# A decoder layer on one core: softmax results turned by VectorE blocks and DMAs through DRAM instead of TensorE transposes

## The chip, the cores and the metric

The kernel runs on one core of a Trainium2 chip. The metric is the time of one execution on the device in microseconds, lower is better. The core has five engines with a queue of instructions each: TensorE (PE, matrix products; PEld are its weight loads), VectorE (DVE), ScalarE (ACT), GpSimd (POOL) and SyncE (SP), which here issues every DMA. Engines wait for each other through semaphores. A DMA adds 16 to its semaphore when it has landed. Products of TensorE land in PSUM, eight banks of 128 x 512 floats; all else lies in SBUF or in DRAM.

## The reference

Eight batches of 128 rows of 512 floats. Three layers, each added to its input: an attention of one head, a cross attention of 32 heads, and a feed forward with a small mixture of low-rank experts. The change is in the cross attention. With `x` normalised and `c` the context, for each head h:

```python
h_q = (x @ w_q.T).reshape(b, lq, H, DH)
h_k = (key_value_states @ w_k.T).reshape(b, lk, H, DH)
h_v = (key_value_states @ w_v.T).reshape(b, lk, H, DH)
score = einsum('bqhd,bkhd->bhqk', h_q, h_k) + position_bias[None]
score = softmax(where(m, score, -inf), axis=-1)
attn = einsum('bhqk,bkhd->bqhd', score, h_v).reshape(b, lq, H * DH)
out = hidden_states + attn @ w_out.T
```

For the product with `h_v` TensorE wants the softmax result of each batch, a 128 x 128 tile with a query in each partition, with a key in each partition: it has to be turned.

## The kernel before, in words

Heads are worked in 16 pairs (`GROUPS`; `PAIR` = 2, head `j` = 0 or 1 of pair `g`). Keys and values of all pairs are projected in a first stage and kept in DRAM (`keys`, `values`); the queries of a pair are projected in the loop, in seven products of a Strassen-like scheme (`project_queries`, slots 0 to 6). Every large product is done in three passes of high and low parts (`three_pass`, L573). The values are written to DRAM in blocks: `turn_blocks` (L1349) turns each 32 x 32 block inside a 128 x 512 tile on VectorE, `store_values` writes them in runs of 128 bytes, `load_values` reads runs of 512 bytes, and so the tile comes back turned as a whole.

Each engine has its order written out by hand, in a function `pair(g)` of its own. On TensorE a pair is: slots 0 to 3 of the queries; the transposes of the probabilities of head (g-1, 1) (`turn_head_probs`, L637); slots 4 to 6; the scores of head (g, 0) (L627); the values of head (g-1, 1) weighed with them (`weigh_head_values`, L645); the scores of head (g, 1); the output products of pair g-1 for six of the eight batches (`project_out`, 48 products in all, in two banks `VO` in turn); the transposes of head (g, 0); the last two batches; the values of head (g, 0).

Between scores and transposes a head goes through `take_scores` (VectorE adds bias and mask, L1210), `maxima` (L1215), `exponentials` (ScalarE, L899), `row_scales` (VectorE, L1229 and L1231) and `normalise_probs` (GpSimd, L534). After the transposes, ScalarE and VectorE copy a bank each to `probs_t` (`copy_probs_t`, L905 and L1236). The weighed values are split into high and low parts (`split_head_out`, L910 and L1241), and `add_out` (L1143) adds the output products to `acc`.

SP issues the DMAs of a pair in `refill(g)`, each behind the wait that frees its buffer: the query weights of the next pair (`fetch_heads`), its bias, the values of this pair (`load_values`, four DMAs of 256 KB), the keys of the next (`load_keys`, 1 MB) and its output weights (`fetch_out`). SP's waits are in order: what stands behind a wait is issued after it.

Of the kernel before, what the change touches and what calls it, by code (L numbers as in the profile page):

```python
# [8 lines left out]
F32 = mybir.dt.float32  # L9
# [3 lines left out]
B = 8  # L13
# [43 lines left out]
def decoder_kernel(nc, x, ctx_t, mask, w_qkv, b_qkv, w_o, b_o, ln_w, pos_bias, weights, w_base, w_routed, w_lora_b,  # L57
                   out):
    with ExitStack() as ctx:
# [63 lines left out]
        probs_t = put("probs_t", ctx_at + 8 * KB, [P, B, P])  # L123
# [33 lines left out]
        beats, ties = (probs_t[:, n:n + 2, :].rearrange("p b (e j) -> p (b e) j", j=NE) for n in (0, 2))  # L157
# [31 lines left out]
        v_loaded = sem("v_loaded")  # L189
        stored = sem("stored")  # L190
# [56 lines left out]
        probs_turned = sem("probs_turned")  # L247
        probs_t0_copied = sem("probs_t0_copied")
# [36 lines left out]
        def _(sp):  # L285
# [105 lines left out]

            fetch_bias(1)
# [3 lines left out]
            fetch_heads(0, 1, Q_COLS)  # L396
            sp.wait_ge(wo_lo_ready, 1)
            fetch_out(1)
            sp.wait_ge(k_stored, 16 * (GROUPS - 2))
            sp.wait_ge(product_done, SLOTS * (K1 + 1))  # L400
            n = 0
            for src, width in ((w_base, KC * C), (w_routed, KC * ROUTED), (w_lora_b, C)):
                sp.dma_start(ffn_raw[:, n:n + width], src).then_inc(ffn_loaded, 16)
                n += width

            def refill(g, last=False):
# [12 lines left out]

            with sp.Fori(1, GROUPS - 1) as g:  # L420
                refill(g)
# [8 lines left out]
        def _(pool):  # L430
# [100 lines left out]
            def normalise_probs(g, j):  # L531
                for i in range(2):
                    pool.wait_ge(scale_ready, 2 * (PAIR * g + j) + i + 1)
                    pool.tensor_tensor(probs[j][:, half(i), :], probs[j][:, half(i), :],  # L534
                                       row_scale[:, j, half(i)].unsqueeze(2).to_broadcast([P, HALF, P]),
                                       ALU.mult).then_inc(probs_ready, 1)
# [30 lines left out]
        def _(pe):  # L567
# [121 lines left out]
            def head_scores(g, j):  # L689
                s = PAIR * g + j + 1  # L690
                for i in range(2):
# [3 lines left out]
            def turn_head_probs(g, j):  # L695
                pe.wait_ge(ot_lo_ready, 2 * (PAIR * g + j + 1))
                turn_probs(PAIR * g + j + 1, probs[j])

            def weigh_head_values(g, j):
                pe.wait_ge(v_loaded, 64 * g + 64)  # L700
                weigh_values(PAIR * g + j + 1, lambda b: v[:, j, b, :], probs_t)

            def project_out(g, some):
                pe.wait_ge(wo_lo_ready, g + 1)
                for b in some:
                    if b % HALF == 0:
                        pe.wait_ge(ot_lo_ready, 2 + 2 * PAIR * g + 3 + b // HALF)
                    pe.wait_ge(out_added, B * (g + 1) + b - 1)
                    three_pass(VO[b % 2][:, :],
                               [([s[:, j, cols(b)] for s in ot], [s[:, j, :] for s in wo])  # L710
                                for j in range(PAIR)]).then_inc(out_done, 1)
# [53 lines left out]
            turn_head_probs(0, 0)  # L765
            weigh_head_values(0, 0)
# [22 lines left out]
            def last_out():  # L789
                g = GROUPS - 1  # L790

                def part(b, j):
                    return three_pass(LAST_OUT[b][:, :], [([s[:, j, cols(b)] for s in ot], [s[:, j, :] for s in wo])],
                                      start=(j == 0), stop=(j == 1))

                pe.wait_ge(wo_lo_ready, GROUPS)
                pe.wait_ge(scores_biased, 2 * HEADS + 2)
                pe.wait_ge(ot_lo_ready, 2 * HEADS)
                pe.wait_ge(dve_took, 3 * (FIRST + GROUPS))
                pe.wait_ge(act_took, 4 * (FIRST + GROUPS))  # L800
                part(0, 0)
                part(1, 0)
                turn_head_probs(g, 1)
                part(2, 0)
                part(3, 0)
                weigh_head_values(g, 1)
                pe.wait_ge(out_added, B * GROUPS)
                part(4, 0)
                part(5, 0)
                for b in range(B):  # L810
# [61 lines left out]
        def _(act):  # L872
# [198 lines left out]

            act.wait_ge(scores_done, 6)
            take(K1, 0, kt)
            take(K1, 1, kt)
            exponentials(1, 0, probs[0], 0)
            take(K1, 2, kt)
            exponentials(1, 0, probs[0], 1)
            high_for_queries(1, (0, 1))
            take(K1, 3, kt)
            high_for_queries(1, (2, 3))  # L1080
            copy_probs_t(1, probs_t)
            exponentials(2, 1, probs[1], 0)
            split_head_out(0, 0)
# [3 lines left out]
            def pair(g, last=False):  # L1087
# [6 lines left out]
                copy_probs_t(PAIR * g, probs_t)  # L1094
# [12 lines left out]
                copy_probs_t(PAIR * g + 1, probs_t)  # L1107
                act.wait_ge(out_done, B * (g + 1))
                high_out(g)
                split_head_out(g, 0)  # L1110
# [7 lines left out]
            copy_probs_t(HEADS, probs_t)  # L1118
# [20 lines left out]
        def _(dve):  # L1139
            def add_out(n, b, banks=None):  # L1140
                dve.wait_ge(out_done, B * n + b + 1)
                of = (banks or VO * HALF)[b]
                dve.tensor_tensor(acc[:, b, :], of[:, :], acc[:, b, :], ALU.add).then_inc(out_added, 1)  # L1143
# [61 lines left out]
            def take_scores(g, j, i):  # L1205
                s = PAIR * g + j + 1
                dve.wait_ge(scores_done, 2 * s + i + 1)
                if i == 0:
                    dve.wait_ge(bias_mask_ready, s)
                dve.tensor_tensor(probs[j][:, half(i), :], tiles(SC[i]), bias_mask[j][:, half(i), :],  # L1210
# [248 lines left out]
            take(K1, 0, kt)  # L1459
            take(K1, 1, kt)  # L1460
            row_scales(0, 0, 0)
            row_scales(0, 0, 1)
            take(K1, 2, kt)
            low_for_queries(1, 0)
            low_for_queries(1, 1)
            copy_probs_t(1, probs_t)
            low_for_queries(1, 2)
            split_head_out(0, 0)
            low_for_queries(1, 3)
            row_scales(0, 1, 0)  # L1470
            row_scales(0, 1, 1)

            def pair(g, last=False):
                n = FIRST + g
                take(n, 0, qt)
                copy_probs_t(PAIR * g, probs_t)
# [11 lines left out]
                for b in range(B):  # L1488
                    add_out(g, b)
                    if b < 2:  # L1490
                        row_scales(g, 0, b)
                    elif b in (2, 3, 4, 6) and not last:
                        low_for_queries(g + 1, (2, 3, 4, 6).index(b))
                    if b in (4, 5):
                        row_scales(g, 1, b - 4)
                    if b == 5:
                        copy_probs_t(PAIR * g + 1, probs_t)
                split_head_out(g, 0)

            with dve.Fori(1, GROUPS - 1) as g:  # L1500
                pair(g)
            pair(GROUPS - 1, last=True)
            copy_probs_t(HEADS, probs_t)
# [145 lines left out]
```

## Time and profile before

| | |
|---|---|
| median of 3 runs | 924.11 us (923.15 to 924.11) |
| profiled execution | 926.98 us, its span 925.3 us |
| TensorE busy | 876.8 us, 95% |
| VectorE busy | 627.8 us, 68% |
| ScalarE busy | 424.4 us, 46% |
| GpSimd busy | 354.0 us, 38% |
| mean granted TensorE clock | 0.991 |
| DMA | 108.52 MB, 117 GB/s over the span |

The span runs from the first to the last instruction of the profiled execution; its own time is 1.7 us longer. A busy share is that of the whole span. Times in the sections below are microseconds from the start of the span.

### The profile page before, as it was taken

How to read it: one execution, taken by the hardware profiler on the slowest of the kernel's cores; microseconds unless marked ns; L12 is line 12 of the kernel's file. 1: busy time of each engine (PE TensorE's matmuls, PEld its weight loads, DVE VectorE, ACT ScalarE, POOL GpSimd, SP SyncE). 2: the span in 40 equal slices, each digit the busy share in tenths (PEclk: the TensorE clock that was granted, in tenths of full speed). 3: DMA queues.
4: the chain of work that ended last, by engine and by line, in shares of the span. 5: the costliest groups of instructions: out<-in, count | busy, mean ns of one | idle time of the engine just before them, and what ended most of it. 6: DMA issues, size and time to landing. Idle time of an engine off the chain costs nothing.

```text
span 925.3 us, 14534 instructions
## 1 busy us (share of the span) xinstructions
PE 876.8 (95%) x4528; PEld 734.8 (79%) x4528; DVE 627.8 (68%) x1086; ACT 424.4 (46%) x1091; POOL 354.0 (38%) x328
## 2 busy tenths in 40 slices
PE   5799998999999999987999999999999999999898
PEld 4677786877777887776888888888888888888697
DVE  7877775677777676566557766677656766576554
ACT  3543443664444344354545553454535554454220
POOL 3312334232443232243764355544554345642100
PEclk9999999999999999999999999999999999999899
DMA  8026565556667657617334342434325352442002
GB/s 272 12 92 153 143 137 140 133 149 157 151 147 183 174 141 141 139 48 175 84 110 128 104 132 71 132 97 135 100 93 136 96 142 74 118 113 45 1 1 91
DMA packets 207661, 108.52 MB, mean 117 GB/s; under 512 B 136592, under 2 KB 187920, under 8 KB 203920
## 3 DMA queue, kind: packets, MB, share of 16 engines
q1 hardware_dynamic: 207632, 108.16, 45.1%
q8 instruction: 15, 0.25, 0.1%
q14 instruction: 14, 0.11, 0.0%
HBM read 74.58 MB, written 33.55 MB: 117 GB/s over the span
## 4 chain that ended last, share of the span: by engine, by line
PE 81%; DVE 10%; issue 3%; POOL 3%; ACT 2%; DMA 1%; SPq 0%; DVEq 0%; ACTq 0%; POOLq 0%
PE bank L573 64%; PE bank L627 6%; PE bank L645 6%; PE bank L637 3%; DVE w_lo L1257 2%; DVE st L1266 1%; DVE turned L1349 1%; PE bank L591 1%; POOL w_sum L477 1%; DMA raw_a<-in_w_qkv 1%; DVE stats L1150 1%; POOL rstd L456 1%; POOL w_sum L475 1%; DVE acc L1143 1%; ACT st L953 1%
## 5 line engine op out<-in xcount | busy, mean ns | idle before, releaser
L953 ACT COPY st<-bank 128x512 f32<-128x512 f32 x192 | 112.2, 587 | 266.0 <-PE bank L573 259.6
L573 PE MATMUL bank<-ctx_hi,w_hi 128*128 128x512 f32 x448 | 179.3, 400 | 16.4 <-DVE st L1266 8.6
L1266 DVE TENSOR_TENSOR st<-bank,st 128x512 f32<-128x512 f32 x144 | 98.4, 689 | 124.9 <-PE bank L573 124.7
L573 PE MATMUL bank<-ctx_lo,w_hi 128*128 128x512 f32 x448 | 174.7, 390 | 0.0
L573 PE MATMUL bank<-ctx_hi,w_lo 128*128 128x512 f32 x448 | 174.7, 390 | 0.0
L475 POOL TENSOR_TENSOR w_sum<-raw 128x256 f32<-128x256 f32 x48 | 39.4, 820 | 251.4 <-PE bank L573 224.0
L534 POOL TENSOR_TENSOR probs<-probs,row_scale 128x512 f32<-128x512 f32 x64 | 66.6, 1040 | 175.7 <-DVE row_scale L1231 172.7
L573 PEld LDWEIGHTS bank<-ctx_hi,w_hi 128*128 128x128 f32 x448 | 84.0, 188 | 46.8 <-issue 11.7
L573 PE MATMUL bank<-wo_hi,ot_hi 128*128 128x512 f32 x256 | 105.3, 412 | 6.5 <-issue 4.7
L1143 DVE TENSOR_TENSOR acc<-bank,acc 128x512 f32<-128x512 f32 x136 | 93.6, 690 | 20.7 <-PE bank L573 18.7
L899 ACT ACTIVATE probs<-probs,neg_max 128x128 f32<-128x128 f32 x264 | 102.4, 392 | 1.1 <-DVE neg_max L1215 1.1
L573 PE MATMUL bank<-wo_lo,ot_hi 128*128 128x512 f32 x256 | 100.9, 394 | 0.0
L573 PE MATMUL bank<-wo_hi,ot_lo 128*128 128x512 f32 x256 | 100.8, 394 | 0.0
L573 PEld LDWEIGHTS bank<-ctx_hi,w_lo 128*128 128x128 f32 x448 | 84.1, 188 | 18.0
L1257 DVE TENSOR_TENSOR w_lo<-w_sum,w_hi 128x512 fp32r<-128x512 f32 x96 | 79.7, 840 | 25.3 <-POOL w_sum L481 19.9
L573 PEld LDWEIGHTS bank<-ctx_lo,w_hi 128*128 128x128 f32 x448 | 84.2, 188 | 15.8
L573 PE MATMUL bank<-x_hi,w_hi 128*128 128x512 f32 x224 | 90.5, 404 | 1.8 <-ACT st L953 1.8
L573 PE MATMUL bank<-x_hi,w_lo 128*128 128x512 f32 x224 | 87.6, 391 | 0.0
L573 PE MATMUL bank<-x_lo,w_hi 128*128 128x512 f32 x224 | 87.6, 391 | 0.0
L498 POOL TENSOR_TENSOR bias_mask<-mask_add,bias 128x1024 f32<-128x1024 f32 x32 | 77.0, 2422 | 11.1 <-DVE probs L1210 11.1
L1257 DVE TENSOR_TENSOR w_lo<-raw,w_hi 128x256 fp32r<-128x256 f32 x96 | 60.1, 626 | 23.2 <-ACT w_hi L945 23.2
L945 ACT CAST w_hi<-w_sum 128x512 fp32r<-128x512 f32 x96 | 59.3, 618 | 14.3 <-POOL w_sum L477 8.1
(135 smaller groups left out, 1528.4 us busy)
## 6 DMA issues: line engine op xcount, KB each, us to landing
raw<-in_weights SPq DMA_DIRECT2D x128, 256.0 KB, 3.1
values<-turned SPq DMA_DIRECT2D x64, 256.0 KB, 4.3
v<-values SPq DMA_DIRECT2D x64, 256.0 KB, 4.7
keys<-st SPq DMA_DIRECT2D x14, 1024.0 KB, 4.9
st<-keys SPq DMA_DIRECT2D x14, 1024.0 KB, 7.3
acc<-in_x SPq DMA_DIRECT2D x8, 256.0 KB, 5.7
ctx_raw<-in_ctx_t SPq DMA_DIRECT2D x4, 512.0 KB, 9.8
bias<-in_pos_bias SPq DMA_DIRECT2D x16, 128.0 KB, 2.1
```

The source lines that it names most:

```text
L475: pool.tensor_tensor(s[:, 1, :], a21, a22, ALU.add).then_inc(w_made[p], 1)
L498: pool.tensor_tensor(bias_mask[j][:, :, :], mask_add[:, :, :], bias[:, j, :].unsqueeze(1).to_broadcast([P, B, P]), ALU.add).then_inc(bias_ ...
L534: pool.tensor_tensor(probs[j][:, half(i), :], probs[j][:, half(i), :], row_scale[:, j, half(i)].unsqueeze(2).to_broadcast([P, HALF, P]), A ...
L573: ins = pe.matmul(out_ap, lhs[a], rhs[b], start=start and k == 0, stop=stop and k == n - 1, skip_group_check=again)
L627: ins = pe.matmul(SC[i][:, cols(t)], q(HALF * i + t), k(HALF * i + t), start=True, stop=True)
L645: ins = pe.matmul(TO[i][:, cols(t)], values_of(b), turned_probs[:, b, :], start=True, stop=True)
L899: ins = act.activation(of[:, b, :], of[:, b, :], ACT.Exp, bias=neg_max[:, j, b:b + 1], accum_out=sums[:, j, b:b + 1])
L945: act.copy(w[p][0][:, at, :], of).then_inc(w_hi_ready[p], 1)
L953: act.copy(to[:, i, j, :], (y, other, y, y)[which][:, :]).then_inc(act_took, 1)
L1143: dve.tensor_tensor(acc[:, b, :], of[:, :], acc[:, b, :], ALU.add).then_inc(out_added, 1)
L1257: dve.tensor_tensor(w[p][1][:, at, :], of, w[p][0][:, at, :].bitcast(F32), ALU.subtract).then_inc(w_lo_ready[p], 1)
L1266: dve.tensor_tensor(to[:, i, j, :], (other, y, other)[which][:, :], to[:, i, j, :], ALU.add).then_inc(dve_took, 1)
```

## The change

TensorE no longer turns the probabilities of the 32 heads. GpSimd writes the normalised probabilities to new tiles `weighed` (half a head each), VectorE turns their 32 x 32 blocks back into `probs[j]` (`turn_probs`), SP writes `probs[j]` to a DRAM tensor `by_blocks` with four DMAs of 128 KB in runs of 128 bytes (`store_blocks`) and, when these have landed, reads it to `probs_t[j]` with four DMAs of 128 KB in runs of 512 bytes (`load_probs_t`). `probs_t` has a tile for each head of the pair now. TensorE weighs the values of head (g, 0) in the next pair, behind slots 0 to 3 of its queries; head (g, 1) stays behind the first scores of the next pair. `project_out` runs in one piece and in a row of eight banks. The weights of the last layer (`fetch_ffn`) are fetched behind the keys of pair 2. VectorE takes `row_scales` ahead of the first `add_out`, and the last two low parts of the query weights at the start of the next pair.

```diff
+        by_blocks = nc.dram_tensor("by_blocks", [PAIR, QUAD, B, 4, 4, QUAD], F32).ap()
+        OUT = VO + TO + SC + VO
...
+            def store_blocks(g, j):
+                sp.wait_ge(blocks_turned, 2 * (PAIR * g + j) + 2)
+                for a in range(4):
+                    sp.dma_start(by_blocks[j, :, :, :, a, :].rearrange("k b c q -> k (b c) q"),
+                                 probs[j][cols(a, QUAD), :, :].rearrange("k b (c q) -> k (b c) q", q=QUAD)
+                                 ).then_inc(blocks_stored[j], 16)
+            def load_probs_t(g, j):
+                sp.wait_ge(blocks_stored[j], 64 * g + 64)
+                if not isinstance(g, int) or g:
+                    sp.wait_ge(pv_done, 2 * PAIR * g + 2 * j)
+                for c in range(4):
+                    sp.dma_start(probs_t[j][cols(c, QUAD), :, :],
+                                 by_blocks[j, :, :, c, :, :].rearrange("k b a q -> k b (a q)")
+                                 ).then_inc(probs_t_loaded[j], 16)
...
             def refill(g, first=False, last=False):
                 if not last:
                     sp.wait_ge(w_lo_ready[0], 4 * (Q_USE + g) + 4)
                     fetch_heads(0, g + 1, Q_COLS)
+                load_probs_t(g - 1, 1)
+                if not last:
                     fetch_bias(g + 1)
                 sp.wait_ge(pv_done, 2 * PAIR * g + 2)
                 load_values(g)
                 if not last:
                     sp.wait_ge(scores_done, 2 * PAIR * g + 6)
                     load_keys(g + 1)
+                if first:
+                    fetch_ffn()
+                store_blocks(g, 0)
+                load_probs_t(g, 0)
+                store_blocks(g, 1)
+                if last:
+                    load_probs_t(g, 1)
+                else:
                     sp.wait_ge(wo_lo_ready, g + 1)
                     fetch_out(g + 1)
...
@@ TensorE, pair(g)
                 project_queries(g, range(4))
-                turn_head_probs(g - 1, 1)
+                weigh_head_values(g - 1, 0)
                 project_queries(g, range(4, SLOTS))
...
                 head_scores(g, 1)
-                project_out(g - 1, range(6))
-                turn_head_probs(g, 0)
-                project_out(g - 1, (6, 7))
-                weigh_head_values(g, 0)
+                project_out(g - 1)
...
@@ VectorE
+            def turn_probs(g, j, i):
+                dve.wait_ge(probs_ready, 2 * (PAIR * g + j + 1) + i + 1)
+                dve.transpose(probs[j][:, half(i), :], weighed[i][:, :, :]).then_inc(blocks_turned, 1)
...
@@ VectorE, pair(g), behind the maxima
+                row_scales(g, 0, 0)
+                row_scales(g, 0, 1)
+                add_out(g, 0)
+                turn_probs(g, 0, 0)
+                add_out(g, 1)
+                turn_probs(g, 0, 1)
+                add_out(g, 2)
+                if not last:
+                    low_for_queries(g + 1, 0)
+                add_out(g, 3)
+                row_scales(g, 1, 0)
+                row_scales(g, 1, 1)
+                add_out(g, 4)
+                if not last:
+                    low_for_queries(g + 1, 1)
+                add_out(g, 5)
+                turn_probs(g, 1, 0)
+                add_out(g, 6)
+                turn_probs(g, 1, 1)
+                add_out(g, 7)
```

## Rows read from the trace of the kernel before

**Rows 1.** Page, part 4: the chain that ended last, by engine.

```profile
PE 81%; DVE 10%; issue 3%; POOL 3%; ACT 2%; DMA 1%; SPq 0%; DVEq 0%; ACTq 0%; POOLq 0%
```

**Rows 2.** The same chain in order of time, one pair: start us, us, what.

```profile
666.19 8.37 PE bank L573 x36
674.56 0.87 PE bank L637 x8
675.43 2.73 PE bank L573 x12
678.17 1.78 PE bank L645 x16
679.95 5.46 PE bank L573 x24
...
686.29 4.10 PE bank L573 x18
```

**Rows 3.** Table by stretch: length; PE, PEld, DVE, ACT, POOL busy; clock; DMA share; GB/s.

```profile
660.00:689.50 29.50, 29.50 (x171) 25.56 (x170) 19.79 (x38) 14.83 (x47) 13.44 (x11) 1.00 0.41 111
```

**Rows 4.** Timeline of SP's queue, the same pair: start us, us, instruction.

```profile
664.57 3.00 SPq L385 DMA_DIRECT2D v<-values  x4
667.84 0.39 SPq L381 DMA_DIRECT2D st<-keys  x1
```

**Rows 5.** Timeline of VectorE and GpSimd behind the second scores of the pair.

```profile
666.86 1.27 DVE L1215 TENSOR_REDUCE neg_max<-probs 128x4 f32<-128x512 f32 x2
...
668.98 0.69 DVE L1143 TENSOR_TENSOR acc<-bank,acc 128x512 f32<-128x512 f32 x1
669.09 2.18 POOL L534 TENSOR_TENSOR probs<-probs,row_scale 128x512 f32<-128x512 f32 x2 [8.14 <-DVE row_scale L1231]
```

**Rows 6.** Timeline of VectorE in the projections: block transposes of the values.

```profile
287.42 2.48 DVE L1349 STREAM_TRANSPOSE turned<-st 128x512 f32<-128x512 f32 x4
```

**Rows 7.** DMA, 664 to 676 in 40 slices; `keys` and `v`, issue to landing.

```profile
GB/s 0 0 0 0 0 0 77 299 311 241 176 210 253 208 212 266 234 195 208 217 198 345 178 288 338 328 355 382 382 410 300 137 82 82 55 27 0 0 0 0
...
st<-keys SPq DMA_DIRECT2D x1, 1024.0 KB, 7.3
...
DMA to landing us min/median/max: 3.6/4.7/5.5
```

**Rows 8.** Stores of values: SP's issues; DMA, 368 to 377 in 40 slices; landing.

```profile
368.36 4.59 SPq L335 DMA_DIRECT2D values<-turned  x4
...
GB/s 0 0 0 0 0 0 0 139 206 204 196 162 175 211 218 217 215 212 165 10 105 209 205 194 172 165 212 218 214 205 201 181 50 127 55 200 291 246 291 428
...
DMA to landing us min/median/max: 3.3/4.2/4.8
```

**Rows 9.** DMA, 681 to 691 in 40 slices: both weight fetches and the bias.

```profile
GB/s 0 0 0 0 0 0 0 49 106 180 336 401 402 385 230 90 131 238 328 295 303 393 205 49 25 25 111 180 221 25 12 0 0 0 0 0 0 0 0 0
```

**Rows 10.** Pair 1: longest wait, pieces of the chain, DMA rate 411.5 to 422.

```profile
POOL w_sum L475 <- DMA raw<-in_weights: 13.2, 1, 13.2
...
421.80 4.73 issue
...
459.55 8.34 PE bank L573 x36
...
DMA packets 1166, 2.97 MB, mean 283 GB/s; under 512 B 115, under 2 KB 302, under 8 KB 1037
```

**Rows 11.** Table by stretch, columns as in rows 3.

```profile
443.55:446.95 3.40, 1.88 (x8) 1.25 (x8) 0.00 (x0) 3.09 (x3) 3.40 (x3) 1.00 0.51 164
...
856.60:860.00 3.40, 1.63 (x10) 1.24 (x9) 1.38 (x2) 0.90 (x2) 2.25 (x1) 1.00 0.00 0
860.00:863.40 3.40, 3.40 (x14) 2.92 (x13) 0.69 (x1) 0.59 (x1) 0.00 (x0) 0.50 0.00 0
```

**Rows 12.** The chain in order of time, behind the last pair's second scores.

```profile
843.40 8.34 PE bank L573 x36
...
864.45 1.78 PE bank L645 x16
```

More of the change, by code:

```diff
@@ L189, in decoder_kernel @@
         v_loaded = sem("v_loaded")
+        blocks_stored = [sem(f"blocks_stored{j}") for j in range(PAIR)]
+        probs_t_loaded = [sem(f"probs_t_loaded{j}") for j in range(PAIR)]
         stored = sem("stored")
@@ L399, in _, with fetch_ffn, refill @@
             sp.wait_ge(k_stored, 16 * (GROUPS - 2))
[L400 to L406, printed above, removed]
+            def fetch_ffn():
+                n = 0
+                for src, width in ((w_base, KC * C), (w_routed, KC * ROUTED), (w_lora_b, C)):
+                    sp.dma_start(ffn_raw[:, n:n + width], src).then_inc(ffn_loaded, 16)
+                    n += width
+            def refill(g, first=False, last=False):
                 if not last:
@@ L416, in refill @@
                     load_keys(g + 1)
+                if first:
[6 more added lines that the diff above has]
+                else:
                     sp.wait_ge(wo_lo_ready, g + 1)
                     fetch_out(g + 1)
-            with sp.Fori(1, GROUPS - 1) as g:
+            refill(1, first=True)
+            with sp.Fori(2, GROUPS - 1) as g:
                 refill(g)
@@ L690, in head_scores @@
                 s = PAIR * g + j + 1
+                if j == 0 and (not isinstance(g, int) or g):
+                    pe.wait_ge(out_added, B * g - 2)
                 for i in range(2):
@@ L693, in head_scores, with project_out @@
                     scores(i, lambda b: qt[:, j, b // HALF, cols(b % HALF)], lambda b: kt[:, j, b // HALF, cols(b % HALF)])
-            def turn_head_probs(g, j):
-                pe.wait_ge(ot_lo_ready, 2 * (PAIR * g + j + 1))
-                turn_probs(PAIR * g + j + 1, probs[j])
             def weigh_head_values(g, j):
+                s = PAIR * g + j + 1
                 pe.wait_ge(v_loaded, 64 * g + 64)
-                weigh_values(PAIR * g + j + 1, lambda b: v[:, j, b, :], probs_t)
-            def project_out(g, some):
-                pe.wait_ge(wo_lo_ready, g + 1)
[L705 to L709, printed above, removed]
+                pe.wait_ge(probs_t_loaded[j], 64 * g + 64)
+                pe.wait_ge(ot_lo_ready, 2 * s)
+                if j == 0:
+                    pe.wait_ge(out_added, B * g + HALF)
+                for i in range(2):
+                    for t in range(HALF):
+                        b = HALF * i + t
+                        ins = pe.matmul(TO[i][:, cols(t)], v[:, j, b, :], probs_t[j][:, b, :], start=True, stop=True)
+                    ins.then_inc(pv_done, 1)
+            def project_out(g):
+                pe.wait_ge(wo_lo_ready, g + 1)
+                for b in range(B):
+                    if b == 0:
+                        pe.wait_ge(ot_lo_ready, 2 + 2 * PAIR * g + 3)
+                        pe.wait_ge(out_added, B * (g + 1))
+                    elif b == 2:
+                        pe.wait_ge(ot_lo_ready, 2 + 2 * PAIR * g + 4)
+                    elif b == 4:
+                        pe.wait_ge(scores_biased, 2 + 2 * PAIR * (g + 2))
+                    elif b >= 6:
+                        pe.wait_ge(out_added, B * (g + 1) + b - 5)
+                    three_pass(OUT[b][:, :],
                                [([s[:, j, cols(b)] for s in ot], [s[:, j, :] for s in wo])
@@ L1458, in _ @@
                     maxima(j + 1, j, probs[j], i)
-            take(K1, 0, kt)
-            take(K1, 1, kt)
             row_scales(0, 0, 0)
             row_scales(0, 0, 1)
+            take(K1, 0, kt)
+            turn_probs(0, 0, 0)
+            take(K1, 1, kt)
+            turn_probs(0, 0, 1)
             take(K1, 2, kt)
@@ L1465, in _, with pair @@
             low_for_queries(1, 1)
[L1466 to L1469, printed above, removed]
             row_scales(0, 1, 0)
             row_scales(0, 1, 1)
-            def pair(g, last=False):
+            low_for_queries(1, 2)
+            low_for_queries(1, 3)
+            turn_probs(0, 1, 0)
+            turn_probs(0, 1, 1)
+            def pair(g, first=False, last=False):
                 n = FIRST + g
+                if not first:
+                    low_for_queries(g, 2)
+                    low_for_queries(g, 3)
                 take(n, 0, qt)
-                copy_probs_t(PAIR * g, probs_t)
+                split_head_out(g - 1, 0)
                 take(n, 1, qt)
@@ L1487, in pair @@
                     maxima(PAIR * g + 2, 1, probs[1], i)
[L1488 to L1500, printed above, removed]
+                row_scales(g, 0, 0)
[18 more added lines that the diff above has]
+                add_out(g, 7)
+            pair(1, first=True)
+            with dve.Fori(2, GROUPS - 1) as g:
                 pair(g)
             pair(GROUPS - 1, last=True)
-            copy_probs_t(HEADS, probs_t)
+            split_head_out(GROUPS - 1, 0)
             split_head_out(GROUPS - 1, 1)
```

44 lines of the change are left out of this document (25 added, 19 removed).

## The prediction

> **What bounds the kernel now.** I read the chain that ended last first. Four fifths of it is TensorE [rows 1]. I then read it in order of time over one pair of heads [rows 2]: every piece is TensorE and each begins where the one before it ends. From one `head_scores(g, 1)` to the next is 29.5 us, and there are fifteen such pairs in the loop. The table by stretch says the same: TensorE is busy for 29.50 of 29.50 us at the full granted clock, VectorE for 19.8, GpSimd for 13.4, and the DMA engines for 0.41 of the time [rows 3]. So a TensorE instruction taken out of the loop is worth its whole duration, as long as nothing that TensorE waits for becomes later.
>
> **What goes.** Per pair, two times eight transposes (L637). One of the two is shown, 0.87 us; the other is as long and stands between the 36 and the 12 output products [rows 2]. Gone with them are the wait of `project_out` for the ping-pong of two banks (36 products take 8.37 us where 24 query products take 5.46, so 0.18 us), and two bank copies each on ScalarE and VectorE, which nothing waited for for long. TensorE alone then needs per pair: 90 products at 5.46/24 = 0.2275 us, 20.5 us; four groups of 16 instructions (two of scores, two of value products) at 1.78 us, 7.1 us; about 0.1 us of switching; 27.7 us in all [rows 2]. That is 1.8 us per pair below 29.5, and 28 us over the kernel.
>
> **What comes.** Call S the moment at which `head_scores(g, 1)` ends and `project_out` begins, 665.9 us by start times in the pair of the rows. The new order needs the turned probabilities of head (g,0) after 48 output and 24 query products, at S + 10.9 + 5.5 = S+16.4, and those of head (g,1) after a value product, 18 query products and a score more: S + 16.4 + 1.8 + 4.1 + 1.8 = S+24.1 [rows 2]. What stands between:
>
> VectorE ends the maxima at S+2.2 [rows 5]. The row scales now come before the first addition. GpSimd starts its two multiplications at S+3.1 now, behind one addition of 0.69 us; without that at S+2.6, ending at S+4.8 [rows 5]. VectorE fits two additions and two block transposes in between. A block transpose of 128x512 is known from `turn_blocks`: four in 2.48 us, 0.62 each [rows 6]. So the blocks of (g,0) are turned at about S+5.8. With eight additions, four transposes and the rest in order, those of (g,1) at about S+12. VectorE's load goes from 19.8 to 19.8 - 2 x 0.69 + 4 x 0.62 = 20.9 us [rows 3, 5, 6]: not a bound.
>
> Then sixteen new DMAs per pair: for each head four stores of 128 KB in 128-byte runs and four loads of 128 KB in 512-byte runs. All go through SP, in order with all others. Nearest rows: four stores of 256 KB in 128-byte runs. Issued from 368.36, they move data from 369.6 to 375.3 [rows 8] and the last lands 4.2 us after its issue at 371.9, 0.9 us behind the data. Half the bytes: 1.2 + 2.9 + 0.9 = 5.0 us. Four loads of 256 KB in 512-byte runs, issued from 664.57 [rows 4], move data from 665.9 to 671.2, and the last lands about 1.2 us later [rows 7]. Half: 1.3 + 2.7 + 1.2 = 5.2 us. Issuing on SP takes about 3 us for four stores (4.59 at double size, [rows 8]) and 2.1 for four loads (3.00 at double size, [rows 4]).
>
> By those alone, head (g,0) would be there at S + 5.9 + 5.0 + 5.2 = S+16.1, just in time. But the same DMA engines carry other transfers. `load_values` and `load_keys` start at S-1.4 and S+1.9 as before. Their data runs without a gap until S+7.5 on most DMA engines and S+9 on the last; the keys land 7.3 us after their issue, at S+9.2 [rows 4, 7]. That one DMA waits behind another is seen in pair 1, where the weights issued behind the 1.8 MB for the last layer hold GpSimd for 13.2 us and TensorE for 4.7 [rows 10]. So I place the first stores behind the keys:
>
> - stores (g,0): data S+8.0 to S+10.9, stored S+11.8
> - loads (g,0): issued S+12.0, data S+13.3 to S+16.0, landed S+17.2: 0.8 us late
> - stores (g,1): SP is free at S+14.2; data behind the loads, S+16.0 to S+18.9, stored S+19.8
> - `fetch_out` and `fetch_heads`, issued before the next loads: 512 KB each, 2.0 us each [rows 9]; data to S+22.9
> - loads (g,1): issued S+20.0, data behind the weights S+22.9 to S+25.6, landed S+26.8.
>
> TensorE wants the last at S+24.1, so it waits 2.7 us per pair in all (0.8 before the first value product, 1.9 before the second), and the pair is 27.7 + 2.7 = 30.4 us against 29.5: 0.9 us longer. Every link is tied to S, so waiting does not work itself off. From S of pair 2 to S of pair 15 there are 13 such periods: +11.7 us. Bounds of this term: with no queueing between transfers the last loads land at about S+24.5 and the pair is 28.1 us (-1.4); with 1.5 us more of straggling in the last three steps it is 31.9 (+2.4). I stay near the middle, since each entry is a measured transfer of the same shape.
>
> A rule of the Trainium skill gives another sum. *DMA: Bandwidth & Descriptors*, section Anatomy of one DMA, puts a transfer at about 2.0 us plus bytes at 436 GB/s: 512 KB would take 3.2 us, store and load together 6.4 instead of 10.2, and all of it would be hidden. Its section Specifications says also that runs below 512 bytes miss line rate. The rows side with the second: 128-byte runs move 1 MB in 5.7 us [rows 8].
>
> **The start.** Between K1 and pair 1 the old order has waits; in the new one the first two chains through DRAM are exposed there, and VectorE's `turn_probs(0, 0, 0)` stands ahead of `take(K1, 1)`. I set S of pair 1 about 2 us later (0 to +5). The 1.8 MB for the last layer now goes behind the keys of pair 2 and ahead of the stores of head (1,0). At 283 GB/s it takes 6.3 us [rows 10]. The loads of pair 1 come 6.3 us later than above: about 9 us of waiting, a pair of 36.7 us, against 459.6 - 421.8 = 37.8 before [rows 10], where the same transfer held TensorE for 4.7 us and a later wait for 1.5 [rows 10, 11]. Together +1 us at S of pair 2.
>
> **The end.** Before, the last value product ends 22.8 us behind the last S [rows 12]. Now, without keys and weights in the way, loads (15,0) land at S+16.1 with no query products to cover them, and loads (15,1) at about S+24, the product ends at S+25.8. Nothing is left to cover the split behind it. +2.4 us, though the wait was already partly there.
>
> **Sum.** +1 + 11.7 + 2.4 = +15.1 us. The profiled execution took 926.98 us (span 925.3, 1.7 around it), 2.9 above the median of 924.11. Added to it that is 942.1; against the median, which the result will be compared with, 939 us.
>
> **Rivals.**
>
> *All hidden (faster), chance 0.27.* The transfers overlap better than one behind the other, or small transfers run faster than half of the double ones. Deciding point: loads (g,1) landed by S+25.9. Below it the pair is shorter than 29.5; at S+24.1 it is 27.7. For it: DMA is busy only 0.41 of a pair [rows 3]. Against it: my chain uses five transfers in series with only 24 us. Price: 13 x -1.8 + 1 + 2.4 = -20, so 904 us; with 0.4 us late, 909. The Trainium skill's fixed cost and rate, above, would give this case.
>
> *The clock falls too, chance 0.16.* At 856.6 TensorE sat idle for 1.8 us and the granted clock of the next stretch was 0.50, that is 1.2 GHz; at 443.6 it sat idle for 1.5 us and stayed at 1.00, 2.4 GHz [rows 11]. My second wait, 1.9 us, is of the same size. Should it bring the fall in every pair, 3.4 us at half rate cost 1.7 us more: 32.1 us per pair, 13 x 2.6 + 3.4 = +37, so 961 us. Against it: in pair 1 and 2 the rows show both outcomes, and the wait is split in two.
>
> *About even, chance 0.12.* Loads land between S+25.2 and S+26.2, 918 to 929 us: what TensorE gains is given back and little more.
>
> *VectorE or GpSimd sets the pace, chance 0.03.* Only if `turn_probs`, queued ahead of `add_out`, holds the banks. But b=6 wants only the first addition, and there are 6 us between. I expect under 0.3 us per pair.
>
> **How the numbers follow.** The likeliest, transfers late by 2.0 to 3.5 us per pair, has 0.42: 939 us, with its own range of 929 to 951. The range 904 to 963 reaches to the hidden case and to the clock case. A change under 0.2% (1.8 us) cannot be told from none. Faster: the hidden case and a quarter of the even one, 0.30. Same: 0.04. Slower: the rest, 0.66.
>
> **What the profile would show.** No L637 in the loop; 27.7 us of TensorE work per pair; in the waits, TensorE's value products held by the DMA into `probs_t`, some 0.8 us for the first head and 1.9 for the second; pairs of 30.4 us; blocks turned near S+5.8; the stores of (g,0) landing near S+11.8, behind the keys; a wait of some 7 us in pair 2; the granted clock at 1.00 in the loop. It would be wrong if the stores don't queue behind the keys, if the loads of (g,1) don't queue behind the weights, or if the clock drops in the loop.

## The result and the profile after

| | before | after |
|---|---|---|
| median, first comparison | 924.11 us (923.15 to 926.38, 4 runs) | 941.89 us (936.53 to 948.72, 4 runs) |
| median, second comparison | 924.93 us (922.83 to 929.84, 13 runs) | 949.28 us (944.24 to 950.72, 4 runs) |
| profiled execution of the first | 926.98 us, span 925.3, clock 0.991 | 936.53 us, span 934.5, clock 0.989 |

The change makes the kernel slower: the ratio of after to before is 1.0186 with a 95% interval of 1.015 to 1.0223, and 1.0248 (1.0204 to 1.0292) in the second comparison. The executions of the new kernel lie further apart than those of the old one. The profiled one is the fastest of them, and it is only 9.2 us of span longer than before.

The page of after, parts 1, 2, 4 and 6:

```profile
PE 855.8 (92%) x4272; PEld 709.6 (76%) x4272; DVE 670.3 (72%) x1118; ACT 408.4 (44%) x1059; POOL 367.8 (39%) x328
...
DMA packets 375596, 142.07 MB, mean 152 GB/s; under 512 B 271760, under 2 KB 355856, under 8 KB 371856
...
PE 39%; SPq 19%; DVE 16%; DMA 12%; issue 8%; POOL 4%; ACT 3%; DVEq 0%; POOLq 0%; ACTq 0%
...
by_blocks<-probs SPq DMA_DIRECT2D x128, 128.0 KB, 3.1
probs_t<-by_blocks SPq DMA_DIRECT2D x128, 128.0 KB, 3.1
```

TensorE's busy time fell by 21 us, and the span still grew. The chain tells why: TensorE had 81% of it [rows 1] and has 39% now; SP's queue and the DMAs, which had 1%, have 31%. The chain no longer follows the products but the probabilities on their way through DRAM. The table by stretch for one pair, columns as in [rows 3]:

```profile
607.60:637.70 30.10, 28.24 (x155) 23.95 (x155) 23.27 (x41) 13.89 (x45) 14.76 (x12) 1.00 0.77 179
```

The pair is 30.1 us long where it was 29.5 [rows 3]. TensorE was busy in all of it and now stands idle for 1.86 us. The DMA engines' share went from 0.41 to 0.77. TensorE's own rows of this pair: start, length, and in brackets the idle time before and what ended it.

```profile
607.57 2.05 PE L758 MATMUL bank<-probs_t,v 128*128 128x128 f32 x16 [0.82 <-DMA probs_t<-by_blocks]
609.45 1.95 PE L676 MATMUL bank<-st,st 128*128 128x128 f32 x16
...
628.24 2.05 PE L758 MATMUL bank<-probs_t,v 128*128 128x128 f32 x16 [0.47 <-DMA probs_t<-by_blocks]
634.26 2.03 PE L676 MATMUL bank<-st,st 128*128 128x128 f32 x16
637.68 2.05 PE L758 MATMUL bank<-probs_t,v 128*128 128x128 f32 x16 [1.39 <-DMA probs_t<-by_blocks]
```

Both value products of a pair (628.24 for the first head, 637.68 for the second) are held by the loads into `probs_t`. The groups themselves are hardly longer than before, where the same view has:

```profile
678.01 1.95 PE L645 MATMUL bank<-probs_t,v 128*128 128x128 f32 x16
```

(The 1.78 us of [rows 2] are pieces of the chain, which end where the next piece begins; the rows of a timeline overlap.) SP's queue over the same pair, where S, the end of the second scores, is 611.2:

```profile
609.79 2.89 SPq L394 DMA_DIRECT2D v<-values  x4
612.93 0.40 SPq L390 DMA_DIRECT2D st<-keys  x1
616.79 3.77 SPq L406 DMA_DIRECT2D by_blocks<-probs  x4
623.02 2.53 SPq L416 DMA_DIRECT2D probs_t<-by_blocks  x4
625.70 2.75 SPq L406 DMA_DIRECT2D by_blocks<-probs  x4
628.63 1.06 SPq L315 DMA_DIRECT2D raw<-in_weights  x2
630.27 0.85 SPq L304 DMA_DIRECT2D raw<-in_weights  x2
631.36 2.55 SPq L416 DMA_DIRECT2D probs_t<-by_blocks  x4
```

And three pieces of the chain in order of time, which say what each of SP's steps waited for:

```profile
619.89 3.12 DMA by_blocks<-probs
623.02 0.58 SPq L416
...
633.30 4.14 DMA probs_t<-by_blocks
637.45 0.23 issue
```

Read together: values and keys at S-1.4 and S+1.7, the stores of head (g,0) at S+5.6, the last of them landed at S+11.8, its loads issued there, the loads of head (g,1) issued at S+20.2, the last landed at 637.45, which is S+26.3. TensorE starts 0.23 us later, at S+26.5. It would have got there at S+24.1, so the pair is 2.4 us longer than the 27.7 us of TensorE's work, and that makes its 30.1.

The end, in the chain behind the last pair's scores:

```profile
850.56 10.91 PE bank L622 x48
861.47 4.57 issue
866.04 3.62 PE bank L758 x16
...
875.49 0.91 PE bank L758 x8
```

TensorE waits 4.57 us for head (15,0), which no query products cover any more. The product then takes 3.62 us, about twice its 1.78 [rows 12]; the granted clock between 866.04 and 869.6 was 0.53. The value product of the last head ends 25.8 us behind S, where it was 22.8.

### The profile page after: what moved, and what is told of

Same layout as the page of the kernel before. It is cut to its first block, busy times and chain, and to the rows that moved or that the text cites. A ratio compares the mean times of both kernels' runs of the same rounds, so it can differ in the third digit from the quotient of the medians.

```text
span 934.5 us, 14353 instructions
## 1 busy us (share of the span) xinstructions
PE 855.8 (92%) x4272; PEld 709.6 (76%) x4272; DVE 670.3 (72%) x1118; ACT 408.4 (44%) x1059; POOL 367.8 (39%) x328
## 2 busy tenths in 40 slices
DMA packets 375596, 142.07 MB, mean 152 GB/s; under 512 B 271760, under 2 KB 355856, under 8 KB 371856
## 4 chain that ended last, share of the span: by engine, by line
PE 39%; SPq 19%; DVE 16%; DMA 12%; issue 8%; POOL 4%; ACT 3%; DVEq 0%; POOLq 0%; ACTq 0%
PE bank L622 32%; SPq L406 9%; SPq L416 6%; DMA probs_t<-by_blocks 6%; DMA by_blocks<-probs 5%; PE bank L758 4%; DVE w_lo L1321 2%; DVE probs L1269 2%; DVE neg_max L1274 2%; DVE turned L1413 2%; SPq L315 2%; POOL weighed L583 1%; PE bank L676 1%; DVE acc L1200 1%; DVE st L1330 1%
## 5 line engine op out<-in xcount | busy, mean ns | idle before, releaser
L622 PE MATMUL bank<-ctx_hi,w_hi 128*128 128x512 f32 x448 | 179.9, 401 | 18.5 <-DVE st L1330 10.3
L583 POOL TENSOR_TENSOR weighed<-probs,row_scale 128x512 f32<-128x512 f32 x64 | 71.7, 1139 | 139.3 <-DVE row_scale L1290 138.9
L622 PEld LDWEIGHTS bank<-ctx_hi,w_hi 128*128 128x128 f32 x448 | 84.4, 188 | 48.9 <-DVE st L1330 11.8
L1321 DVE TENSOR_TENSOR w_lo<-raw,w_hi 128x256 fp32r<-128x256 f32 x96 | 91.3, 951 | 23.2 <-ACT w_hi L1006 23.2
L622 PE MATMUL bank<-wo_hi,ot_hi 128*128 128x512 f32 x256 | 101.2, 395 | 2.0 <-DVE ot_lo L1305 2.0
L1321 DVE TENSOR_TENSOR w_lo<-w_sum,w_hi 128x512 fp32r<-128x512 f32 x96 | 82.0, 864 | 25.4 <-POOL w_sum L526 19.9
L758 PE MATMUL bank<-probs_t,v 128*128 128x128 f32 x512 | 68.0, 288 | 32.2 <-DMA probs_t<-by_blocks 24.9
L758 PEld LDWEIGHTS bank<-probs_t,v 128*128 128x128 f32 x512 | 62.5, 199 | 41.4 <-issue 41.1
L1200 DVE TENSOR_TENSOR acc<-bank,acc 128x512 f32<-128x512 f32 x136 | 90.6, 669 | 0.9 <-PE bank L622 0.9
L1305 DVE TENSOR_TENSOR ot_lo<-bank,ot_hi 128x512 fp32r<-128x512 f32 x66 | 45.7, 692 | 63.3 <-ACT ot_hi L971 63.2
```

Of the source, the lines that this page charges most:

```text
L583: pool.tensor_tensor(weighed[i][:, :, :], probs[j][:, half(i), :], row_scale[:, j, half(i)].unsqueeze(2).to_broadcast([P, HALF, P]), ALU.m ...
L622: ins = pe.matmul(out_ap, lhs[a], rhs[b], start=start and k == 0, stop=stop and k == n - 1, skip_group_check=again)
L758: ins = pe.matmul(TO[i][:, cols(t)], v[:, j, b, :], probs_t[j][:, b, :], start=True, stop=True)
L1305: dve.tensor_tensor(lo(i), TO[i][:, :], hi(i).bitcast(F32), ALU.subtract).then_inc(ot_lo_ready, 1)
L1321: dve.tensor_tensor(w[p][1][:, at, :], of, w[p][0][:, at, :].bitcast(F32), ALU.subtract).then_inc(w_lo_ready[p], 1)
```

## The experiments

Experiments 2 and 3 leave out the new DMAs or half of their bytes and bound the loss, 4, 5 and 7 move single transfers, and 6, 8, 9 and 10 look for a version that wins. "Waits" below are TensorE's for `probs_t` between 470 and 830 us, as the list of waits has them: 23.4 us in after, 23 times; none at all before.

**1. The same kernel once more.** No edit.

> The changed kernel once more, for its spread. In its first four executions the span went from 934.5 to 946.8 us while the mean granted TensorE clock went from 0.989 to 0.978. If the spread comes from stretches at half clock (theory: the waits of TensorE in the loop are of the size that sometimes brings the clock down), a slower execution again shows a lower mean clock: about 1.7 us more for each 0.0018 less. If the spread comes from the transfers alone, time and clock are not related. Time 936 to 949 us.

Measured: 949.28 us, ratio 1.0248 (1.0204 to 1.0292), span 947.9, mean clock 0.978. Executions with a lower mean clock took longer by and large, as expected, but not at the rate that was named: 944.24 us had 0.987, nearly the 0.989 of the 936.53 us before. So the clock is only a part of the spread. Two stretches of this profiled execution, columns as in [rows 3], and TensorE's row where the clock falls:

```profile
548.50:551.90 3.40, 1.39 (x13) 1.21 (x12) 2.57 (x4) 0.48 (x2) 2.53 (x4) 1.00 0.70 123
551.90:555.30 3.40, 3.40 (x16) 3.40 (x17) 0.69 (x1) 0.59 (x1) 0.32 (x1) 0.50 0.00 0
```

```profile
551.82 3.68 PE L758 MATMUL bank<-probs_t,v 128*128 128x128 f32 x16 [2.01 <-DMA probs_t<-by_blocks]
```

TensorE waited 2.01 us in the first stretch, and in the next the granted clock was 0.50, that is 1.2 GHz; the sixteen instructions took 3.68 us. The same stands at 644.0 behind a wait of 2.10 us, and no fall followed a wait of 2.01 us at 706.0 or one of 2.31 us at 767.9. The two pairs with these falls took 32.3 and 31.7 us, their neighbours 29.8 to 30.3. From the last scores of pair 2 to those of pair 15 this execution took 400.4 us, the first one 392.0.

**2. No trip through DRAM.** `store_blocks` and `load_probs_t` are empty, and TensorE reads the half-turned tile, so the kernel leaves out a part of the turning. VectorE's wait for earlier stores goes with them.

```diff
-                pe.wait_ge(probs_t_loaded[j], 64 * g + 64)
+                pe.wait_ge(blocks_turned, 2 * (PAIR * g + j) + 2)
...
-                        ins = pe.matmul(TO[i][:, cols(t)], v[:, j, b, :], probs_t[j][:, b, :], start=True, stop=True)
+                        ins = pe.matmul(TO[i][:, cols(t)], v[:, j, b, :], probs[j][:, b, :], start=True, stop=True)
```

> The stores to by_blocks and the loads to probs_t are left out; TensorE waits for the block transposes and takes the half-turned tiles from probs[j], so the result is not the reference's. Order of all engines as in the changed kernel. Theory (five transfers in series behind each S are late): without them a pair is TensorE's work alone, 27.7 to 27.9 us instead of 30.2, about 895 us in all, with no wait in the value products. Rival (the new order of engine work costs the time, VectorE's transposes ahead of the additions for example): pairs stay above 29 us, and the time above 915 us.

Measured: 895.71 us, ratio 0.9675 (0.9643 to 0.9707). One pair:

```profile
537.90:565.60 27.70, 27.70 (x156) 24.01 (x156) 22.56 (x40) 13.82 (x46) 15.13 (x11) 1.00 0.43 118
```

27.70 us, all of it TensorE at the full clock. So TensorE's own work is what the prediction said, and VectorE's block transposes, its new order and GpSimd's cost nothing in the loop. What makes the pairs of after long is in the sixteen DMAs.

**3. Half the bytes in as many DMAs.** Stores and loads move four of the eight batches, and TensorE takes these four for both halves.

```diff
-                    sp.dma_start(probs_t[j][cols(c, QUAD), :, :],
-                                 by_blocks[j, :, :, c, :, :].rearrange("k b a q -> k b (a q)")
+                    sp.dma_start(probs_t[j][cols(c, QUAD), 0:HALF, :],
+                                 by_blocks[j, :, 0:HALF, c, :, :].rearrange("k b a q -> k b (a q)")
```

> Each store and load moves four of the eight batches, TensorE takes these tiles for both halves, so the result is not the reference's. As many DMAs in the same order, half the bytes. Theory (time of the data in the line): stores and loads take 1.4 us less each, the last loads land at about S+22, no wait is left, 27.7 us a pair, about 903 us. Rival (what costs is the fixed part of a DMA, issue and completion): waits of at least 1 us stay, 29 us a pair or more, 920 us or more.

Measured: 899.33 us, ratio 0.9707 (0.9681 to 0.9732), pairs of 27.7 us and no wait. SP's queue, for an S of 651.07:

```profile
656.70 1.95 SPq L406 DMA_DIRECT2D by_blocks<-probs  x4
661.51 1.73 SPq L416 DMA_DIRECT2D probs_t<-by_blocks  x4
...
668.78 1.75 SPq L416 DMA_DIRECT2D probs_t<-by_blocks  x4
```

The stores start at S+5.6 as before, are stored 1.4 us earlier (S+10.4), and the last loads are issued at S+17.7 in place of S+20.2. The number of DMAs is the same, so it is not a fixed cost of each DMA that makes the loads late, but something that grows with what they move. The run does not say what: packets fall with the bytes (those under 512 B from 271760 to 206225 over the execution), and SP issues four stores in 1.95 us in place of 3.77.

**4. The output weights behind the loads.** `fetch_out` moves from ahead of the loads of head (g,1) to behind them.

```diff
                 load_probs_t(g - 1, 1)
+                if not first:
+                    sp.wait_ge(wo_lo_ready, g)
+                    fetch_out(g)
...
-                else:
-                    sp.wait_ge(wo_lo_ready, g + 1)
-                    fetch_out(g + 1)
```

> Only the place of fetch_out in SP's order: behind the loads of head (g,1) instead of ahead of them. The same bytes. Theory (transfers stand in one line): the loads of (g,1) land 2 us earlier, about S+24.3, the second wait goes, the first (0.3 to 0.8 us) stays, a pair is 28.8 to 29.1 us and the time about 922 us. Rival (the DMA engines are short of bandwidth over the whole pair, whatever the order): under 0.3 us per pair, 932 us or more.

Measured: 925.96 us (10 runs), ratio 1.0009 (0.9982 to 1.0037): level with before. The waits fall from 23.4 to 9.4 us. The last loads are issued at S+19.8, hardly earlier than S+20.2, but 512 KB less stands ahead of them.

**5. The keys in two halves.** Half of `load_keys` goes behind the stores of head (g,0).

```diff
-                    load_keys(g + 1)
+                    load_keys(g + 1, 0)
...
                 store_blocks(g, 0)
+                if not last:
+                    load_keys(g + 1, 1)
                 load_probs_t(g, 0)
```

> Only the keys in two halves, the second behind the stores of head (g,0); fetch_out stays ahead of the loads of (g,1). Theory: the first wait of TensorE goes; the chain behind it gets about 1 us earlier, but its loads still stand behind both weight fetches and come at about S+25, so a wait of some 0.9 us stays: pairs of about 28.9 us, some 922 us. Rival (only the weights matter): as the changed kernel, 30 us.

Measured: 927.54 us (10 runs), ratio 1.0017 (0.9988 to 1.0045); waits 16.1 us in 13 pieces where there were 23. The waits of the first head are gone but for one of 0.43 us, those of the second stay. The loss is all but gone, for 512 KB moved past the stores.

**6. Both moves.**

> As out_late, and the 1 MB of keys in two halves, the second behind the stores of head (g,0), in the time in which these land. Theory: the stores of (g,0) come 1.9 us earlier, their loads land at about S+16 and the first wait goes too; a pair is 28.0 to 28.5 us, the time 908 to 914 us, below the kernel before. Rival (the first stores don't queue behind the keys): as out_late, about 922 us.

Measured: 908.64 us, ratio 0.9841 (0.9802 to 0.9881); in a later comparison of 5 rounds 912.06 us, 0.9846 (0.9813 to 0.9878). The chain and SP's queue over one pair:

```profile
682.11 16.36 PE bank L624 x72
698.47 1.78 PE bank L760 x16
700.25 4.09 PE bank L624 x18
704.35 1.86 PE bank L678 x16
...
```

```profile
632.05 2.78 SPq L406 DMA_DIRECT2D by_blocks<-probs  x4
635.01 0.54 SPq L390 DMA_DIRECT2D st<-keys  x1
636.92 2.53 SPq L416 DMA_DIRECT2D probs_t<-by_blocks  x4
639.60 2.77 SPq L406 DMA_DIRECT2D by_blocks<-probs  x4
...
644.92 2.55 SPq L416 DMA_DIRECT2D probs_t<-by_blocks  x4
```

The chain is TensorE alone again, piece on piece: 16.36 us for 72 output and query products, 27.7 us for the pair, waits of 0.8 us in all between 470 and 830 (2.2 us in the later comparison's execution). With S at 626.4, the first loads go at S+10.5 and the second at S+18.5 (after: S+11.8 and S+20.2). Every byte of after is still moved. So the waits come from what stands ahead in the line, not from the load of the DMA engines as such.

What is left is the end. TensorE's row behind its last products:

```profile
836.06 2.26 PE L760 MATMUL bank<-probs_t,v 128*128 128x128 f32 x9 [4.70 <-issue]
```

A wait of 4.70 us, and from 834.7 the granted clock was 0.50 for 10.2 us.

**7. The keys from ScalarE's queue.** A second queue might let the stores pass the keys. All else is as in after.

```diff
+                if not last:
+                    act.wait_ge(scores_done, 2 * PAIR * g + 6)
+                    act.dma_start(kt[:, :, :, :].rearrange("p i j n -> p (i j n)"), keys[g + 1]).then_inc(k_loaded, 16)
```

> The keys are issued by ScalarE, at the same moment within 0.5 us (behind the exponentials of the first head), all else as in the changed kernel. If a transfer waits because it stands behind another in SP's own queue, the stores of (g,0) no longer wait for the keys: stored at S+11 or earlier, first wait gone, pairs about 29.3 us, 926 us. If it waits because the 16 DMA engines are shared whoever issues, nothing changes: 30.2 us a pair, 936 to 949 us. I expect the second, with the keys landing later than S+9.2 since both move together.

Measured: 959.27 us, ratio 1.0341 (1.0297 to 1.0384). Both expectations missed. SP's queue, S at 617.5, and the table of DMA issues between 606 and 636:

```profile
623.08 4.53 SPq L406 DMA_DIRECT2D by_blocks<-probs  x4
630.17 2.53 SPq L416 DMA_DIRECT2D probs_t<-by_blocks  x4
```

```profile
v<-values SPq DMA_DIRECT2D x4, 256.0 KB, 6.4
st<-keys ACTq DMA_DIRECT2D x1, 1024.0 KB, 8.1
```

The last column is the time from issue to landing. In after it is 4.5 us for the values and 7.1 for the keys in the same stretch. ScalarE issues the keys at 617.86, which is S+0.4, where SP did at S+1.7. So they move beside more of the values and hold them up. They take longer themselves and land at S+8.5 in place of S+8.9, not later than S+9.2 as I had expected. The stores are issued at S+5.6 as before and are stored at S+12.7 in place of S+11.8. Waits grow to 30.2 us, and six value products of the loop take 2.49 to 3.55 us, at mean granted clocks of 0.54 to 0.79. How much of the loss comes from the queue and how much from the earlier moment of issue was not separated. The two queues share the same engines. The Trainium skill says so in *DMA: Bandwidth & Descriptors*, section Issuing engines are not separate DMA queues; by it the move gains nothing but issue time. The run goes beyond it: its ratio lies 0.9 and 1.6 points above those of the two comparisons of after.

**8. Both moves, and the split of the last layer's weights a pair later.** In pair 1, ScalarE waits for the 1.8 MB of those weights and queries wait for ScalarE.

```diff
-            act.wait_ge(ffn_loaded, 48)
-            act.copy(ffn[0][:, :], ffn_raw[:, :]).then_inc(ffn_hi_ready, 1)
+            pair(2, ffn_here=True)
```

> As both, and the split of the last layer's weights (a wait for their DMA, 3.2 us of ScalarE and 7.9 us of GpSimd) one pair later, on ScalarE in a gap in front of high_out. Theory: pair 1 to pair 2 goes from 32.4 us to about 28 us, 4 us less in all, about 904.5 us. Rival (that stretch is long because the block transfers stand behind the 1.8 MB): no change, 908.6 us.

Measured: 913.83 us, ratio 0.985 (0.981 to 0.989), no gain over both. With that wait gone the transfer itself is next, as SP's queue in pair 1 shows:

```profile
435.54 5.99 SPq L406 DMA_DIRECT2D by_blocks<-probs  x4
...
444.18 2.53 SPq L416 DMA_DIRECT2D probs_t<-by_blocks  x4
```

The stores take 8.6 us from first issue to stored, where those of an ordinary pair of after take 6.2, and the value product waits 2.60 us and falls to half clock. In experiment 6 the stores of this pair take 8.7 us, but there the wait for ScalarE hid it. Besides, the last scores of pair 1 end 3.8 us later than in experiment 6 (429.5 against 425.7), because the value product at 423.34 waited 3.66 us, where it waited 1.68 us in experiment 6.

**9. Both moves, and the last pair turned on TensorE.** In pair 15 GpSimd normalises into `probs`, and the eight transposes of before come back, at their old places for head 0 and among the last output products for head 1.

```diff
+                if last:
+                    project_out(g - 1, range(6))
+                    pe.wait_ge(out_added, B * g + HALF)
+                    turn_last(0)
+                    project_out(g - 1, (6, 7))
```

> As both, and in the last pair alone TensorE turns the probabilities of both heads, as in the kernel before (in it the chain through DRAM has no query products of a next pair to hide behind: the first value product waited 4.7 us, and a stretch at half clock of 10.2 us followed). Theory: from the last S to the last value product 22 to 23 us instead of 26.9, without the slow stretch behind it; 4 to 6 us less, 903 to 905 us. Rival (the end is set by the additions and statistics of VectorE): no change.

Measured: **904.16 us** (902.25 to 905.03), ratio 0.9771 (0.9745 to 0.9797), and 7.9 us under both in the same comparison. The chain behind the last scores:

```profile
821.49 8.20 PE bank L622 x36
829.69 0.87 PE bank L686 x8
830.57 2.75 PE bank L622 x12
...
840.82 1.78 PE bank L771 x16
```

The last value product ends 21.1 us behind S; before it was 22.8 [rows 12], in after 25.8. No half clock stands there, and the mean clock is 0.996. This version beats both kernels, the old one by 2.3%.

**10. The same, and the 1.8 MB in four pieces in pairs 2 to 5.**

```diff
+                if isinstance(g, int) and 2 <= g <= 5:
+                    fetch_ffn(g - 2)
...
-                if first:
-                    fetch_ffn()
```

> As both_tail, and the 1.8 MB for the last layer in four pieces of at most 512 KB behind the bias of pairs 2 to 5, their split on ScalarE and GpSimd in and behind pair 5. Theory (the 1.8 MB in front of the stores of pair 1, and ScalarE's wait for them, make pair 1 to pair 2 32.4 us): 28 to 29 us there, under 0.5 us lost in each of four pairs; 3 us less than both_tail, about 901 us. Rival: the pieces delay the values and the chain of each of the four pairs by their 1.8 us, and nothing is gained.

Measured: 904.24 us, ratio 0.9766 (0.974 to 0.9793), the same as without. From S of pair 1 to S of pair 2 it takes 28.8 us instead of 33.1. But TensorE now waits 4.04 us at 422.6, ahead of pair 1's last scores, so that S of pair 2 stands at 457.3 as without the edit (457.6), and the pairs from there to S of pair 15 take 1.5 us more. The early wait is in every execution, 2.71 us long in experiment 9 and 1.68 in 6. What sets its length was not tried.

## Why the prediction was right

Forecast: 939 us with a range of 904 to 963; measured 941.89 and 949.28. In the ordinary pairs of the loop the mechanism held link by link; in pair 1 it did not, and the clock fell where it should have stayed. The sizes, for the profiled execution:

| step | predicted | measured |
|---|---|---|
| TensorE alone, per pair | 27.7 us | 27.70 (no trip through DRAM) |
| blocks of (g,0) turned | S+5.8 | S+5.6 |
| stores of (g,0) stored | S+11.8 | S+11.8 |
| SP free for the next stores | S+14.2 | S+14.5 |
| loads of (g,1) issued, landed | S+20.0, S+26.8 | S+20.2, S+26.3 |
| pair | 30.4 us | 30.16 (392.0 / 13) |
| pairs 2 to 15 | +11.7 us | +8.2 |
| S of pair 1, S of pair 2 | +2, +1 | +1.6, -1.0 |
| end | +2.4 us | +2.0 |
| sum | +15.1 us | +9.2 (span) |

*What comes.* The step "I place the first stores behind the keys" was the one that decided, and experiments 5 and 6 show it: with half the keys moved away, the first wait goes. The second, `fetch_out` ahead of the loads of (g,1), is shown by experiment 4. Each move alone wins back the loss, both together the whole 1.8 us of a pair. Against the rival that a DMA's fixed cost makes the chain, half the bytes (experiment 3) gives no wait at all.

*The sum.* It was 5.9 us too large for this execution. 3.5 us of that are the pairs. The first of the thirteen took 33.0 us, with a wait of 2.42 us and a fall of the clock; the last took 28.5, with no query weights ahead of its loads. The eleven between take 30.05 on average: the loads of (g,1) landed 0.5 us earlier than my series of transfers had them, and the 0.23 us from landing to start were not in it. The end was 0.4 us too large.

*Pair 1.* The other 2.0 us are the start: pair 1 took 35.1 us against the 36.7 predicted and began 0.4 us earlier. The size is near, but by luck. I had some 9 us of waiting for the loads behind the 1.8 MB. The trace of after has only 1.05 us of it, ahead of the second value product, and before that a wait for ScalarE:

```profile
436.34 3.18 ACT L1171 CAST ffn_hi<-ffn_raw 128x3584 fp32r<-128x3584 f32 x1 [0.94 <-DMA ffn_raw<-in_w_lora_b]
440.06 0.79 PE L622 MATMUL bank<-x_hi,w_hi 128*128 128x512 f32 x1 [3.03 <-ACT st L1014]
```

ScalarE takes the 1.8 MB in as soon as they land, and the copy that a query product waits for stands behind it. The rest is the clock, which was 0.50 from 440.0 to 445.9, about 2.9 us more than at the full clock. With TensorE that late, the first value product at 445.34 waited for nothing. Of the 7.4 us above 27.7 the step that I named is 1.05.

*The clock.* As an event in every pair the rival was wrong; in single pairs it was right, and the prediction's own sign of being wrong, a clock that drops in the loop, came. The first profiled execution shows the fall in pair 1 and one from pair 2 to 3, at 487.1 behind the wait of 2.42 us; the second has both, and two more behind waits of 2.01 and 2.10 us. The length of the wait alone does not decide: no fall followed 2.11 us at 518.0 of the first execution, 2.48 in experiment 5 or 3.31 in experiment 7, and one followed 1.98 in experiment 4. The medians, 17.8 and 24.4 us above before, lie further up than the fastest execution, which is 12.4 us above the median of before, and longer executions have by and large the lower mean clock (0.989 at 936.5, 0.983 at 940.0, 0.985 at 943.8, 0.978 at 948.7). I named the mechanism with a wait of 1.9 us for every pair; waits of about that size bring it now and then. So the median met the forecast in part because deviations cancelled: the sum was some 6 us too large for the fastest execution, and the clock was left out of the likeliest case. Of the 8.4 us by which the loop of the second execution is longer, 3.2 are the two value products at half clock (3.68 and 3.66 against 2.05) and 4.8 are longer waits (28.2 against 23.4 between 470 and 830 us); why these differ between executions stays open.

*VectorE.* 20.9 us were predicted, 23.3 measured. The term that was mis-sized is the place of a low part of the query weights. Before, it ran beside an idle GpSimd, and after, beside GpSimd's split of the output weights. First a row of VectorE's timeline of before, then the timeline of both engines in after:

```profile
677.46 0.68 DVE L1257 TENSOR_TENSOR w_lo<-raw,w_hi 128x512 fp32r<-128x512 f32 x1
```

```profile
623.58 2.56 POOL L549 TENSOR_TENSOR wo_lo<-raw,wo_hi 128x1024 fp32r<-128x1024 f32 x1 [2.38 <-ACT wo_hi L1125]
623.81 2.88 DVE L1321 TENSOR_TENSOR w_lo<-raw,w_hi 128x512 fp32r<-128x512 f32 x1
```

The same instruction takes 2.88 us in place of 0.68, and ends 0.5 us behind GpSimd's. These 2.2 us are nearly the whole difference. It is so in every pair of the loop of after, and before never above 0.69 us there; no run moves the instruction back to test it. VectorE's load in experiment 2 is 22.6 us and its pairs are 27.7, so it cost nothing.

*All hidden.* The rival's price was right (904 us) and its condition wrong for this order of transfers: the loads landed at S+26.3, behind its deciding point of S+25.9. With the order of experiment 6 it comes true. The sum by the formula of the Trainium skill's page *DMA: Bandwidth & Descriptors*, section Anatomy of one DMA, was an estimated 3.2 us for the 512 KB of a store or a load. That section gives the formula for single DMAs issued by GpSimd, and I had put it on four in a row issued by SP. The trace disagrees: 6.2 us for the stores of (g,0) behind the keys, 6.1 for the loads of (g,1) behind the weights, and 5.0 for the loads of (g,0) (issued from 623.02, TensorE starts on them at 628.24), which have no other transfer ahead. The measurement decides.

## What to carry to other kernels

When work moves from an engine to DMAs, draw the line of transfers over one period and ask what stands ahead of each new one; a busy share of 0.41 said nothing about that, and the order in the queue was worth 3 to 4 points here at the same bytes. A transfer whose data is wanted a period later (keys, weights) belongs behind the chain that is wanted now, and moving it to another queue does not do that. The first and last periods have no cover: there the old way may stay the better one, as in the last pair here.

## What the runs showed of the hardware

- TensorE started 0.23 us after the landing of the DMA that it waited for.
- TensorE waits of 1.98, 2.01, 2.10, 2.20 and 2.42 us were followed by half the granted clock; others of 2.01, 2.11, 2.31, 2.48 and 3.31 us were not.
- A VectorE subtraction of 128x512 floats took 2.88 us beside a GpSimd subtraction of 128x1024, and 0.68 us with GpSimd idle.
- With 1 MB issued from a second engine's queue, 1.3 us sooner, the 256 KB loads of the first landed after 6.4 us in place of 4.5, and the 1 MB after 8.1 in place of 7.1.
